# One matmul for both halves' output shift, and the experts' scale and shift spread once: a routed-expert layer on one Trainium2 core

## The reference, cut to what matters

```python
def _expert_ffn(xf, Wi_e, bi_e, Wg_e, bg_e, Wo_e, bo_e, g_e, b_e):
    h = gelu(xf @ Wi_e + bi_e) * sigmoid(xf @ Wg_e + bg_e)
    r = xf + (h @ Wo_e + bo_e)
    mu = mean(r); var = mean(square(r - mu))
    return (r - mu) * rsqrt(var + EPS) * g_e + b_e

x = L0_attn_x                                   # 16 x 512 x 128, float32
x = x + attention(layernorm(x))                 # 16 heads of 8, causal
probs = softmax(layernorm(x) @ Wr + br); the two largest of 8 experts, weights renormalised
x = x + sum over the two experts of weight * expert(layernorm(x))
```

## Time and profile before

| | |
|---|---|
| median of 3 runs | 1240.49 us (1239.62 to 1243.29) |
| the profiled execution, its own time | 1241.94 us |
| its span in the trace | 1240.2 us, 27505 instructions |
| busy: PE, PEld, DVE, ACT, POOL | 1105.6, 835.8, 982.0, 796.9, 741.8 us |
| attention | 0 to about 771 us |
| tail | about 771 to 812 us |
| experts, 71 blocks | about 812 to 1198 us |
| combine | about 1202 to 1238 us |

### The profile page before, as it was taken

The page is one execution under the profiler, slowest core; times in us unless marked ns, Lnnn a source line. Parts: engine busy times, 40 slices in busy tenths (PEclk is TensorE's granted clock), DMA queues, the critical chain, the costliest instruction groups (busy, mean ns, idle before and its releaser), DMA issues. The chain is left out here.

```text
span 1240.2 us, 27505 instructions
## 1 busy us (share of the span) xinstructions
PE 1105.6 (89%) x8654; PEld 835.8 (67%) x8654; DVE 982.0 (79%) x2792; ACT 796.9 (64%) x1800; POOL 741.8 (60%) x1359
## 2 busy tenths in 40 slices
PE   3899999999999999999999998179999999999930
PEld 1565655665656666666666664079999999999920
DVE  4777778788788788788878873758888888888859
ACT  2465665675666666666666565268888888888810
POOL 2257475675576576576576566716666666666640
PEclk9999999999999999999999998579999999999975
DMA  5223545434434434433433421521111111111138
GB/s 145 94 77 113 168 135 166 130 93 125 130 101 125 129 109 123 131 105 113 142 112 93 138 60 36 171 53 53 52 53 54 53 53 53 53 53 53 32 123 305
DMA packets 138270, 127.38 MB, mean 103 GB/s; under 512 B 71848, under 2 KB 96432, under 8 KB 138128
## 3 DMA queue, kind: packets, MB, share of 16 engines
q1 hardware_dynamic: 127184, 103.59, 28.7%
q0 software_dynamic: 8640, 17.84, 4.4%
q10 hardware_dynamic: 2304, 4.20, 0.9%
HBM read 71.13 MB, written 54.43 MB: 101 GB/s over the span
## 5 line engine op out<-in xcount | busy, mean ns | idle before, releaser
L808 ACT ACTIVATE probs<-st 128x384 f32<-128x384 f32 (+1 forms) x768 | 389.1, 525 | 204.9 <-PE st L704 181.8
L849 DVE TENSOR_REDUCE neg_max<-sa 128x2 fp32r<-128x1024 f32 (+3 forms) x384 | 395.6, 1036 | 135.1 <-PE sa L689 126.9
L642 POOL TENSOR_SCALAR_AFFINE_SELECT probs<-probs 128x128 f32<-128x128 f32 (+1 forms) x768 | 245.5, 332 | 243.1 <-ACT probs L808 232.6
L704 PE MATMUL st<-q_stack,k_pad 128*128 128x256 f32 (+2 forms) x1024 | 338.4, 372 | 15.6 <-DMA q_stack<-max_scratch 9.1
L684 PE MATMUL sa<-k_pad,q_stack 128*128 128x256 f32 (+2 forms) x1024 | 328.1, 363 | 12.8 <-DVE neg_max L849 6.7
L684 PEld LDWEIGHTS sa<-k_pad,q_stack 128*128 128x128 f32 x1024 | 178.0, 192 | 111.8 <-issue 69.8
L704 PEld LDWEIGHTS st<-q_stack,k_pad 128*128 128x128 f32 x1024 | 177.2, 192 | 48.4 <-ACT probs L808 20.9
L1006 POOL DMA_INDIRECT y_scratch<-z,to_row x142 | 170.7, 1202 | 35.9 <-issue 35.9
L1040 PE MATMUL up<-xt_hi,w_cur 128*128 128x256 f32 x568 | 167.7, 295 | 0.0
L717 PE MATMUL pv<-probs,v_aug 128*32 128x512 f32 (+3 forms) x2048 | 167.1, 445 | 0.0
L1041 PE MATMUL up<-xt_lo,w_cur 128*128 128x256 f32 x568 | 161.6, 285 | 0.0
(11 more groups left out here) (160 smaller groups left out, 1477.2 us busy)
## 6 DMA issues: line engine op xcount, KB each, us to landing
q_stack<-q_scratch SPq DMA_DIRECT2D x64, 256.0 KB, 2.6
k_pad<-k_scratch SPq DMA_DIRECT2D x256, 64.0 KB, 2.5
xg<-rows_scratch SPq DMA_DIRECT2D x71, 130.0 KB
q_scratch<-q_hi SPq DMA_DIRECT2D x16, 512.0 KB, 3.1
k_scratch<-k_hi SPq DMA_DIRECT2D x16, 512.0 KB, 2.9
y<-y_scratch SPq DMA_DIRECT2D x16, 512.0 KB, 5.3
q_scratch<-q_lo SPq DMA_DIRECT2D x17, 256.0 KB, 3.1
k_scratch<-k_lo SPq DMA_DIRECT2D x17, 256.0 KB, 3.1
```

The costliest lines, as they stand in the source:

```text
L642: pool.affine_select(out=blk, in_=blk, compare_op=ALU.is_ge, fill=0.0, base=0, pattern=[[0, w], [1, P]], channel_multiplier=-1).then_inc(m ...
L704: last = nc.tensor.matmul(st[:, t % 2, at:at + w], k_pad[:, G * g + j, kk * P:(kk + 1) * P], q_stack[:, g, S - w:S], start=True, stop=True)
L808: nc.scalar.activation(probs[:, n % 2, j, lo:lo + w], st[:, k % 2, at:at + w], ACT.Exp).then_inc(exp_done, 1)
L849: V.tensor_reduce(neg_max[:, n % 2, heads[0]:heads[-1] + 1, i], scores[:, :, 0:(i + 1) * P], AX.X, ALU.max, negate=True).then_inc(sa_read, 1)
```

## The change

Four steps `GBa` to `GBd` come into the tail behind `BU`. Each lets TensorE spread gamma and beta of two experts into `misc` (two matmuls of 256 columns), and ScalarE copies that into a new SBUF tile `gb_sb` with all 8 experts' gamma and beta on all partitions. They take part in the turns on `misc`, so `CM-` now waits for the fourth copy. In the experts, `gamma_beta` is gone, and `scale` and `shift` read `gb_sb` at the place of the block's expert, which a register gives. `y_ps` is one tile for both halves: one matmul of 256 columns (the same 128 columns of `b_stack` read twice) starts both, and the products of both halves add to it.

```diff
-        LAST = """PD BU AR Rc- Rd- CM- Re- Rf- W0 W1 W2 out ln2 S0- rs2 zn S1- W3 W4 W5 W6 zT W7 W8 LG LGa S2- S3- Ra EX
+        LAST = """PD BU GBa GBb GBc GBd AR Rc- Rd- CM- Re- Rf- W0 W1 W2 out ln2 S0- rs2 zn S1- W3 W4 W5 W6 zT W7 W8 LG LGa S2- S3- Ra EX
...
+        gb_sb = sb("gb_sb", [P, E * 2 * D])
...
+                elif kind in GB_STEPS:
+                    misc_free(pe, kind, n)
+                    pe.wait_ge(r_const, made["b_stack, b_sel"])
+                    for half in range(2):
+                        e = 2 * GB_STEPS.index(kind) + half
+                        last = nc.tensor.matmul(misc[:, half * 2 * D:(half + 1) * 2 * D], b_sel[:, e * P:(e + 1) * P],
+                                                b_stack[:, D:3 * D], start=True, stop=True)
+                    last.then_inc(misc_written, 1)
...
+                if kind in GB_STEPS:
+                    i = GB_STEPS.index(kind)
+                    act.wait_ge(misc_written, misc_use(kind, n))
+                    act.wait_ge(pv_written, GROUPS_ALL)
+                    nc.scalar.activation(gb_sb[:, i * 4 * D:(i + 1) * 4 * D], misc[:, :], ACT.Copy).then_inc(gb_done, 1)
...
-        y_ps = [pb(f"y_ps{h}", [P, D]) for h in range(2)]
+        y_ps = pb("y_ps", [P, 2, D])
...
+                nc.tensor.matmul(y_ps[:, :, :], b_sel[:, bass.ds(e * P, P)],
+                                 b_stack[:, 0:D].unsqueeze(1).broadcast_to([P, 2, D]), start=True, stop=True)
                 for h in range(2):
-                    nc.tensor.matmul(y_ps[h][:, :], b_sel[:, bass.ds(e * P, P)], b_stack[:, 0:D],
-                                     start=True, stop=False)
                     for c in range(FC):
-                        last = nc.tensor.matmul(y_ps[h][:, :], hid[:, u % 2, c, h * P:(h + 1) * P],
+                        last = nc.tensor.matmul(y_ps[:, h, :], hid[:, u % 2, c, h * P:(h + 1) * P],
                                                 wo_sb[:, bass.ds(e * (FC * D) + c * D, D)],
-                                                start=False, stop=(c == FC - 1))
+                                                start=False, stop=True, skip_group_check=True)
...
-            def gamma_beta(s, u):
-                e = expert_of(u)
-                if not before(s, 1):
-                    pe.wait_ge(z_done, s)
-                nc.tensor.matmul(gb_ps, b_sel[:, bass.ds(e * P, P)], b_stack[:, D:3 * D],
-                                 start=True, stop=True).then_inc(gb_written, 1)
...
             def scale(s, u):
-                dve.wait_ge(gb_written, s + 1)
                 for h in range(2):
                     last = V.scalar_tensor_tensor(z[:, r, h, :], res[:, r, h, :], mean_var[:, r, h, 0:1],
-                                                  gb_ps[:, 0:D], ALU.subtract, ALU.mult)
+                                                  gb_sb[:, bass.ds(e * (2 * D), D)], ALU.subtract, ALU.mult)
...
             def shift(s, u):
                 for h in range(2):
                     last = V.scalar_tensor_tensor(z[:, r, h, :], z[:, r, h, :], inv_dev[:, r, h:h + 1],
-                                                  gb_ps[:, D:2 * D], ALU.mult, ALU.add)
+                                                  gb_sb[:, bass.ds(e * (2 * D) + D, D)], ALU.mult, ALU.add)
```

More of the change, by code:

```diff
@@ L184, in attention_and_routed_experts @@
         w_hi_done, w_lo_done = sem("w_hi_done"), sem("w_lo_done")
+        gb_done = sem("gb_done")
         pads_made, runs_done, pads_stored = sem("pads_made"), sem("runs_done"), sem("pads_stored")
@@ L238, in attention_and_routed_experts @@
         ORDER, TAIL = list(schedule()), list(tail())
-        MISC_USERS = ("xT", "Q", "K", "V", "zT", "LG", "CM", "BU")
+        GB_STEPS = ("GBa", "GBb", "GBc", "GBd")
+        MISC_USERS = ("xT", "Q", "K", "V", "zT", "LG", "CM", "BU") + GB_STEPS
         MISC_ORDER = [(kind, n) for kind, _, n in ORDER + TAIL if kind in MISC_USERS]
@@ L396, in misc_free @@
                                "V": (vaug_done, b_ + 1), "zT": (zT_done, b_ + 1), "LG": (logits_done, b_ + 1),
-                               "CM": (rank_done, b_ + 1), "BU": (b_up_done, 1)}[before]
+                               "CM": (rank_done, b_ + 1), "BU": (b_up_done, 1),
+                               **{step: (gb_done, i + 1) for i, step in enumerate(GB_STEPS)}}[before]
                 pe.wait_ge(done, count)
@@ L625, in constants @@
                                                             base=0, pattern=[[-1, E], [0, P]], channel_multiplier=1))
+                    made["b_stack, b_sel"] = count["const"]
             for kind, k, n in ORDER:
@@ L812, in _ @@
                 act_sequence(act, kind, k, n)
-                if kind == "W":
+                if kind in GB_STEPS:
[3 more added lines that the diff above has]
+                    nc.scalar.activation(gb_sb[:, i * 4 * D:(i + 1) * 4 * D], misc[:, :], ACT.Copy).then_inc(gb_done, 1)
+                elif kind == "W":
                     e, m = k // 2, k % 2
@@ L933, in attention_and_routed_experts @@
         up = pb("up", [P, 4, F])
-        y_ps = [pb(f"y_ps{h}", [P, D]) for h in range(2)]
+        y_ps = pb("y_ps", [P, 2, D])
         xt_ps = pb("xt_ps", [P, BR])
-        gb_ps = misc[:, 0:2 * D]
         gathered = [sem(f"gathered{u}") for u in range(NX)]
@@ L942, in attention_and_routed_experts @@
         up_written, up_read = sem("up_written"), sem("up_read")
-        hid_done, gb_written = sem("hid_done"), sem("gb_written")
+        hid_done = sem("hid_done")
         y_written, res_done, ve_done, dev_done = sem("y_written"), sem("res_done"), sem("ve_done"), sem("dev_done")
@@ L1049, in down @@
                     pe.wait_ge(res_done, s)
+                nc.tensor.matmul(y_ps[:, :, :], b_sel[:, bass.ds(e * P, P)],
+                                 b_stack[:, 0:D].unsqueeze(1).broadcast_to([P, 2, D]), start=True, stop=True)
                 for h in range(2):
-                    nc.tensor.matmul(y_ps[h][:, :], b_sel[:, bass.ds(e * P, P)], b_stack[:, 0:D],
-                                     start=True, stop=False)
                     for c in range(FC):
-                        last = nc.tensor.matmul(y_ps[h][:, :], hid[:, u % 2, c, h * P:(h + 1) * P],
+                        last = nc.tensor.matmul(y_ps[:, h, :], hid[:, u % 2, c, h * P:(h + 1) * P],
                                                 wo_sb[:, bass.ds(e * (FC * D) + c * D, D)],
-                                                start=False, stop=(c == FC - 1))
+                                                start=False, stop=True, skip_group_check=True)
                 last.then_inc(y_written, 1)
-            def gamma_beta(s, u):
-                e = expert_of(u)
-                if not before(s, 1):
-                    pe.wait_ge(z_done, s)
-                nc.tensor.matmul(gb_ps, b_sel[:, bass.ds(e * P, P)], b_stack[:, D:3 * D],
-                                 start=True, stop=True).then_inc(gb_written, 1)
-            stages(pe, [(0, up_projections), (0, load_expert), (1, down), (-2, transpose_x), (2, gamma_beta)])
+            stages(pe, [(0, up_projections), (0, load_expert), (1, down), (-2, transpose_x)])
         @block.scalar
@@ L1141, in residual @@
                 for h in range(2):
-                    last = V.scalar_tensor_tensor(res[:, u % NR, h, :], y_ps[h][:, :], 0.5, xg[:, u, h, 0:D],
+                    last = V.scalar_tensor_tensor(res[:, u % NR, h, :], y_ps[:, h, :], 0.5, xg[:, u, h, 0:D],
                                                   ALU.mult, ALU.add)
@@ L1163, in scale @@
             def scale(s, u):
-                r = u % NR
+                e, r = expert_of(u), u % NR
                 if s >= NR:
                     dve.wait_ge(scattered[r], rounds(s - NR, NR, 32))
-                dve.wait_ge(gb_written, s + 1)
                 for h in range(2):
                     last = V.scalar_tensor_tensor(z[:, r, h, :], res[:, r, h, :], mean_var[:, r, h, 0:1],
-                                                  gb_ps[:, 0:D], ALU.subtract, ALU.mult)
+                                                  gb_sb[:, bass.ds(e * (2 * D), D)], ALU.subtract, ALU.mult)
                 last.then_inc(z_chain, 1)
             def shift(s, u):
-                r = u % NR
+                e, r = expert_of(u), u % NR
                 dve.wait_ge(z_chain, s + 1)
```

## The result

The changed kernel takes 1224.62 us (median of 4 runs, 1221.78 to 1226.38) against 1240.05 us (median of 4 runs, 1238.72 to 1243.29) for the kernel before, run beside it: 0.987 of the time, 95% interval 0.9841 to 0.9898. The forecast was 1232.2 us with a range from 1229.0 to 1237.5.

What follows compares the result with a forecast made beforehand. The prediction took TensorE's own work in the experts as the bound: 7.6 us saved from gamma_beta plus 0.7 from the shift product, 0 for the tail, 8.3 in all, from 1240.49 to 1232.2 us, range 1229.0 to 1237.5.

Steps and rivals of the forecast that it cites:

- TensorE is the bound: In the experts, TensorE waits for nobody and its own work sets the step of 5.21 us.
- gamma_beta, 0.11 us a step: In TensorE's expert steps, removing this product saves 0.11 us in each of 69 steps, 7.6 us.
- One shift product, 0.01 us a step: In TensorE's expert steps, one 256-column product replacing two saves 0.01 us a step, 0.7 us in 70 steps.
- that leaves 0.07 and 0.05, together 0.12: Cost of the two old shift products per expert step, after subtracting 0.95 us of float32 instructions from each half.
- The upper bound: Largest gain allowed for the single shift product: 0.05 us a step, +3.5 us, as if doubled width were free.
- scale and shift out of SBUF, 0.19 us more for VectorE, hidden: In the experts, VectorE gets 0.09 + 0.10 us more a step; its wait shrinks to 0.26 us and hides it.
- the register step behind the wait: On VectorE, shift's register step cannot run ahead of the wait for scale: 0.10 us, bounds 0 and 0.25.
- VectorE takes over: Rival in the experts: VectorE's step reaches 5.19 us, saving only 1.4 us, time 1239.1; chance 0.10 for partial takeover.
- becomes the bound: Rival "slower than before" in the experts: a longer hold makes VectorE's step 5.48 us, 19 us more, 1259; chance 0.04.
- The hold of scale by a scatter: In the experts, scale with two SBUF inputs waits for GpSimd's second scatter: 0.21 us, or up to 1.03 us.
- The tail costs nothing: The four spreading steps in the tail, 1.2 us each, cost 0, at most 2 us; rival that it shows: 0.07.
- the covers named: In the tail, GpSimd's memset holding VectorE, then VectorE's 1.15 us idle before the last batch's statistics, hide the later counts.

Runs made afterwards that it cites:

- e1: The kernel before with only the single 256-column shift product in one PSUM tile, gamma_beta kept in each step; 1232.36 us, 0.9929 of before.
- e8: The changed kernel run again, unaltered; 1223.57 us, 0.987 of the kernel before.
- e2: The changed kernel with two 128-column shift products and two PSUM tiles as before, gamma and beta spread once; 1233.24 us, 0.9933 of before.
- e7: The changed kernel with eight spreading steps in the tail, the last four repeating the first four; 1227.66 us, 0.9897 of before.
- e9: The changed kernel with two separate 128-column shift products in one tile, and each half's first float32 weight load halved; 1271.26 us, 1.0274 of before.
- e10: The changed kernel, its 256-column shift product kept, with each half's first float32 weight load halved; 1270.79 us, 1.0265 of before.

## Why the prediction was wrong, point by point

**TensorE is the bound: right.** It waits for nobody before or after, and in e1 to e8 the step follows its stream.

**gamma_beta, 0.11 us a step: right.** 0.106 in e2.

**One shift product, 0.01 us a step: wrong, by 0.10 us in each of 70 steps, 7 us in all.** The step that failed is "that leaves 0.07 and 0.05, together 0.12". The forecast took the 0.95 us from the first float32 instruction to the next shift product as the time of the eight, and set them at 0.119 us each. They take 0.11 each once the stream runs, 0.89 in all; the other 0.05 to 0.06 us are the wait for the float32 weight load that the narrow product ahead is too short to cover, and this shows only in the distance from the first to the second instruction behind it. So the pair cost 0.12 + 0.11 = 0.23 us, of which 0.12 are left: 0.11 saved, as e1 measured (0.108). The upper bound failed with it: it was put at 0.05 us, "the whole second product, as if the doubled width were free", while the whole second product was 0.11. With 0.11 in place of the 0.01, the sum is 7.6 + 7.7 = 15.3 us, and the forecast 1225.2. The trace of before held the answer: in windows so narrow that each float32 instruction has its own row, the first spacing is 0.16 us and the rest 0.11. The forecast read the eight as one merged row of "x8".

**scale and shift out of SBUF, 0.19 us more for VectorE, hidden: right in kind, too high.** At equal steps of 5.10 us VectorE waits 35.0 us in 62 steps in e1 (PSUM) and 26.9 in 62 in e2 (SBUF): 0.13 us more work. Between the kernel before and the changed one it is hardly anything, 5.21 - 0.57 = 4.64 us against 4.99 - 0.34 = 4.65. What makes the two differ was not tried; 0.19 is too high by either. In the changed kernel, VectorE's timeline is

```profile
1002.36 0.61 DVE L1178 SCALAR_TENSOR_TENSOR z<-res,mean_var,gb_sb 128x128 f32<-128x128 f32 x2
1002.88 0.24 DVE L1165 BATCH_NORM_AGGREGATE mean_var<-st 128x2 f32<-128x6 f32 x2
1003.12 0.61 DVE L1187 SCALAR_TENSOR_TENSOR z<-z,inv_dev,gb_sb 128x128 f32<-128x128 f32 x2
1003.65 0.16 DVE L1170 TENSOR_SCALAR inv_dev<-mean_var 128x2 f32<-128x2 f32 x1
```

scale 0.52 (as before), shift 0.53 (0.49), and shift starts 0.24 us behind the mean where it was 0.16: 0.08 us that the register step behind the wait would explain, in the guessed size; no run changes it alone. Neither the 0.26 us less that the Trainium skill, VectorE: DVE Perf Modes, would give nor the full 0.09 us more shows.

**VectorE takes over, or becomes the bound: did not happen.** It keeps 0.34 us a step. The hold of scale by a scatter, on which both rivals rest, is not there. From 835 to 1150 us, 123 of the 126 instructions of scale in the changed kernel start while a scatter is under way, and the longest of all takes 349 ns:

```profile
L1178 DVE SCALAR_TENSOR_TENSOR z<-res,mean_var,gb_sb x126: 337/343/349, 837.6 to 1147.4; 128x128 f32<-128x128 f32 x126
```

GpSimd's scatters are longer, 1365 ns in the mean against 1218 before, but 1115 in e2, which reads the same operands, so the operands alone are not the reason; what sets their length was not tried, and GpSimd has idle time for it.

**The tail costs nothing: right,** with the covers named, and with the order in which they are used up shown by e7.

**The chances.** 0.86 for faster was fair. The range failed at the low end because its bound for the shift product, 0.05 us, was less than half of the 0.11 us that the second product cost.

## What to carry to other kernels

In a stream of float32 products with 128 weight columns, a short product in a cheaper type is not paid by its columns. Below about 0.11 us of streaming it costs 0.11 to 0.12 us anyway, because the float32 load behind it takes that long, unless what stands behind it needs no float32 weights. So put such products together, up to 256 bfloat16 columns for the price of 128, or next to each other. And cost an instruction in a pipeline by what the stream is without it, as with gamma_beta at block 1, not by the distance to the next start: the price may show one instruction later. Where loads have rows of their own, read those too.

## What the runs showed of the hardware that was not expected

- A bfloat16 product of 128 columns costs 0.06 us ahead of another such, and 0.11 to 0.12 us ahead of a float32 one; one of 256 columns 0.12, one of 512 columns 0.23 (0.113 more). All at the full granted clock.
- Behind the start of a float32 load of 128 weight columns the next load starts after 0.108 us at the earliest, in all twelve traces; behind one of 64 columns after 0.055 (e9, e10); behind a bfloat16 one of 128 after 0.005.
- Two float32 instructions with 64 weight columns ahead of six with 128, in each half of a block (e9, e10), made a step 0.57 and 0.67 us longer, though they load and write less.
- VectorE's instruction of three inputs took 343 and 349 ns with gamma and beta in SBUF, and 342 and 329 with them in PSUM: for this operation and size the place matters by 0 to 20 ns.
- The attention stage, unchanged, ended anywhere between 766.8 and 774.0 us in twelve profiled executions, while two executions of the changed kernel agree in the experts' step to 0.001 us.
